# A graph attention layer with a routed expert layer: ScalarE's step in another order, and one penalty as a square

## What is computed

```python
# graph layer, on h = layernorm(x)
e_k   = leaky_relu((h * a_k) @ h.T, 0.2)          # k = 0..3
alpha = where(adj == k + 1, e_k, -9e15)           # one of four scores, or the penalty
x     = x + softmax(alpha) @ h
# expert layer, on layernorm(x): softmax gate over 16 experts, the best two,
# silu(x @ w1) * (x @ w2) @ w3 of each, weighted and added
```

## Time and profile before

| | |
|---|---|
| median of three runs | 921.12 us |
| profiled execution, its own time | 917.78 us |
| its span, first to last instruction | 915.6 us |
| TensorE busy | 732.7 us (80%) |
| VectorE busy | 518.6 us (57%) |
| GpSimd busy | 527.9 us (58%) |
| ScalarE busy | 382.3 us (42%) |
| mean granted TensorE clock | 0.939 |
| DMA | 133.26 MB, mean 146 GB/s |

### The profile page before, as it was taken

The page is one execution under the profiler, slowest core; times in us unless marked ns, Lnnn a source line. Parts: engine busy times, 40 slices in busy tenths (PEclk is TensorE's granted clock), DMA queues, the critical chain, the costliest instruction groups (busy, mean ns, idle before and its releaser), DMA issues.

```text
span 915.6 us, 17656 instructions
## 1 busy us (share of the span) xinstructions
PE 732.7 (80%) x4422; PEld 593.4 (65%) x4423; DVE 518.6 (57%) x1770; ACT 382.3 (42%) x947; POOL 527.9 (58%) x668
## 2 busy tenths in 40 slices
PE   4898988888898647887878878888788887888873
PEld 2455556555555536776767778777777777877873
DVE  4899999999999844444444444443333332333331
ACT  6878787878787212222222222222222222222220
POOL 3348877777777765554554554454564554544553
PEclk9999999999999858998999999999999998999987
DMA  5324453322221035766765544628755555555610
GB/s 151 93 81 143 120 145 119 110 85 90 87 83 34 28 112 173 216 202 209 233 210 180 165 163 147 208 95 245 226 174 182 179 178 187 168 163 173 205 58 1
DMA packets 127460, 133.26 MB, mean 146 GB/s; under 512 B 16362, under 2 KB 98545, under 8 KB 127378
## 3 DMA queue, kind: packets, MB, share of 16 engines
q1 hardware_dynamic: 107008, 94.66, 34.2%
q0 software_dynamic: 15616, 34.38, 11.0%
q10 hardware_dynamic: 4754, 3.25, 1.2%
HBM read 52.28 MB, written 41.19 MB: 102 GB/s over the span
## 4 chain that ended last, share of the span: by engine, by line
PE 64%; issue 17%; ACT 12%; another core or an unknown queue 3%; DVE 1%; POOL 1%; DMA 0%; POOLq 0%; ACTq 0%; DVEq 0%
PE psS L1124 30%; PE bank L1148 14%; ACT late L628 6%; PE bank L1040 4%; ACT late L636 4%; PE bank L1138 4%; PE psS L1012 3%; PE bank L1071 3%; PE bank L995 2%; PE bank L1024 2%; ACT h L645 1%; PE bank L1032 1%; POOL out_dram L593 1%; PE bank L1059 1%
## 5 line engine op out<-in xcount | busy, mean ns | idle before, releaser
L1124 PE MATMUL psS<-xT,late 128*128 128x256 f32 (+1 forms) x1280 | 269.9, 362 | 100.1 <-issue 87.0
L1124 PEld LDWEIGHTS psS<-xT,late 128*128 128x128 f32 x1280 | 213.0, 205 | 128.1 <-issue 98.5
L964 DVE TENSOR_TENSOR hid<-silu,psS 128x512 f32<-128x512 f32 x144 | 99.0, 687 | 239.5 <-PE psS L1124 108.4
L581 POOL DMA_INDIRECT second_list<-xin x144 | 142.4, 989 | 139.3 <-DVE xin L977 99.0
L593 POOL DMA_INDIRECT out_dram<-xin x144 | 141.5, 983 | 133.0 <-DVE xin L977 93.5
L667 ACT ACTIVATE silu<-psS 128x512 f32<-128x512 f32 x144 | 86.0, 597 | 298.7 <-PE psS L1124 171.6
L569 POOL DMA_INDIRECT first_list<-stage,slot x128 | 133.3, 1041 | 47.7 <-issue 36.0
L1148 PE MATMUL bank<-wts,hid 128*128 (+1 forms) x1152 | 159.7, 284 | 0.4 <-issue 0.3
L977 DVE SCALAR_TENSOR_TENSOR xin<-bank,xin 128x128 f32<-128x128 f32 x288 | 87.4, 345 | 109.5 <-remote 83.1
L1148 PEld LDWEIGHTS bank<-wts,hid 128*128 128x128 f32 x1152 | 148.1, 201 | 0.7 <-issue 0.7
L1012 PE MATMUL psS<-late,hT 128*128 128x512 f32 x256 | 117.4, 601 | 2.8 <-ACT late L628 2.8
(11 more groups left out here) (154 smaller groups left out, 812.5 us busy)
## 6 DMA issues: line engine op xcount, KB each, us to landing
late<-wts SPq DMA_DIRECT2D x160, 256.0 KB
xin<-second_list SPq DMA_DIRECT2D x48, 262.0 KB
X<-in_x_dram SPq DMA_DIRECT2D x32, 256.0 KB
late<-in_adj_dram SPq DMA_DIRECT2D x32, 256.0 KB
xin<-first_list SPq DMA_DIRECT2D x48, 134.0 KB
xin<-second_list SPq DMA_DIRECT2D x48, 131.0 KB
wts<-in_L_ffn_w_dram SPq DMA_DIRECT2D x48, 128.0 KB
xin<-first_list SPq DMA_DIRECT2D x48, 67.0 KB
```

The source lines that it names most:

```text
L581: pool.indirect_dma_start(second_list[:, :], bass.IndirectOffsetOnAxis(ap=xin[:, u, k, SLOT1:SLOT1 + 1].bitcast(i32), axis=0), xin[:, u, k ...
L964: v.tensor_tensor(hid[:, w, :], silu[:, w, :], psU[w], ALU.mult).then_inc(s_hid[u % TURNS], 1)
L1124: last = mm(out[:, c * W2 + rows.start:c * W2 + rows.stop], at[:, half * H + c * P:half * H + (c + 1) * P], xT[:, w, rows], start=True, st ...
```

## The change

ScalarE's order within a step: before it is `adjb(s)`, small exponential, `hT` and `hTa`, exponentials, `h(s+1)`, `probT`, `x1T`. Now it is small exponential, square, `hT` and `hTa`, exponentials, `adjb(s+1)`, `probT`, `x1T`, `h(s+1)`. So the bf16 copy of a group is made one step sooner, and `h` last.

The square: the penalty for k = 0 is made by ScalarE as `(2^28 * adj - 2^28)^2`, which is zero where `adj` is 1, read straight from the integer tile. VectorE makes the other three, as `(adj != k+1) * 2^56`. All four are positive now and TensorE subtracts them: the identity of the penalty matmul is replaced by its negative, `minusb`. The load of `adj` is released by the square's semaphore in place of the copy's.

```diff
-    NEG_INF = -9e15
+    ROOT = 2.0 ** 28
+    SQUARES = 1
...
             def load_adj(g):
-                wait(sp, s_adjb, g - 1)
+                wait(sp, s_squares, g - 1)
...
+            for k in range(SQUARES):
+                nc.gpsimd.memset(shift[:, k:k + 1], -ROOT * (k + 1)).then_inc(s_const, 1)
...
-                if on(0):
-                    act.wait_ge(s_adj[s % 2], (s // 2 + 1) * 16)
-                    wait(act, s_pen, s)
-                    nc.scalar.activation(adjb, adjt[:, s % 2, :], ACT.Copy).then_inc(s_adjb, 1)
                 if pair(s, 6) is not None:
...
+                if on(0):
+                    act.wait_ge(s_adj[s % 2], (s // 2 + 1) * 16)
+                    wait(act, s_S, s - 1)
+                    for k in range(SQUARES):
+                        last = nc.scalar.activation(pen[:, s % 2, k, :], adjt[:, s % 2, :], ACT.Square,
+                                                    scale=ROOT, bias=shift[:, k:k + 1])
+                    last.then_inc(s_squares, 1)
...
                 if on(-1):
                     g = s + 1
-                    act.wait_ge(s_sh, s + 2)
-                    wait(act, s_O, g - HB + 1)
-                    for t in range(T):
-                        last = nc.scalar.activation(h[:, g % HB, t * D:(t + 1) * D], X[:, g % XQ, t * D:(t + 1) * D],
-                                                    ACT.Identity, scale=norm[:, b, 0, t, 0:1],
-                                                    bias=norm[:, b, 0, t, 1:2])
-                    last.then_inc(s_h, 1)
+                    act.wait_ge(s_adj[g % 2], (g // 2 + 1) * 16)
+                    wait(act, s_pen, g)
+                    nc.scalar.activation(adjb, adjt[:, g % 2, :], ACT.Copy).then_inc(s_adjb, 1)
...
+                if on(-1):
+                    g = s + 1
+                    act.wait_ge(s_sh, s + 2)
+                    wait(act, s_O, g - HB + 1)
+                    for t in range(T):
+                        last = nc.scalar.activation(h[:, g % HB, t * D:(t + 1) * D], X[:, g % XQ, t * D:(t + 1) * D],
+                                                    ACT.Identity, scale=norm[:, b, 0, t, 0:1],
+                                                    bias=norm[:, b, 0, t, 1:2])
+                    last.then_inc(s_h, 1)
...
-                v.tensor_copy(identb[:, :], ident[:, :]).then_inc(s_base, 1)
+                v.tensor_scalar(minusb[:, :], ident[:, :], -1.0, None, ALU.mult).then_inc(s_base, 1)
...
-                    for k in range(K):
-                        last = v.tensor_scalar(pen[:, s % 2, k, :], adjb, float(k + 1), NEG_INF / SLOPE,
+                    for k in range(SQUARES, K):
+                        last = v.tensor_scalar(pen[:, s % 2, k, :], adjb, float(k + 1), ROOT * ROOT,
                                                ALU.not_equal, ALU.mult)
...
                     pe.wait_ge(s_pen, g + 1)
+                    pe.wait_ge(s_squares, g + 1)
                     for t in range(T):
-                        last = mm(psS[:, t, :], identb[:, :], pen[:, g % 2, :, t * D:(t + 1) * D],
+                        last = mm(psS[:, t, :], minusb[:, :], pen[:, g % 2, :, t * D:(t + 1) * D],
                                   start=False, stop=True)
```

More of the change, by code:

```diff
@@ L101, in gnn_then_moe @@
         pen = late[:, (K + 6) * C:(2 * K + 6) * C].bitcast(bf16).rearrange("p (q k c) -> p q k c", q=2, k=K)
-        identb = sb("identb", [P, P], bf16)
+        minusb = sb("minusb", [P, P], bf16)
         stats = sb("stats", [P, 2, 2, T, 3])
@@ L106, in gnn_then_moe @@
         norm = sb("norm", [P, 2, 2, T, 2])
+        shift = sb("shift", [P, SQUARES])
         minus_half = sb("minus_half", [P, 2, T])
@@ L235, in gnn_then_moe @@
         s_pen = sem("s_pen")
+        s_squares = sem("s_squares")
         s_sel = sem("s_sel")
@@ L295, in gnn_then_moe @@
         s_z = [sem(f"s_z{i}") for i in range(S)]
-        CONSTS = 10
+        CONSTS = 11
         AT = 2 * T * E
```

## The result

The changed kernel takes 914.26 us as the median of 17 runs (908.37 to 928.53), the kernel before 921.12 beside it (17 runs, 909.38 to 932.88). The ratio is 0.9936, with 95% interval 0.9909 to 0.9964: faster by 0.64%, where the forecast was 906.7, a ratio of 0.9843. The ratio is taken without the executions that ran over 1.5% above the fastest of their kernel, so it isn't the quotient of the two medians (0.9926). The time lies outside the forecast's range of 903.3 to 912.5. The profiled execution has a span of 912.4 us and took 914.26.

The account below looks back on a forecast made before the run. A TensorE-ScalarE loop bound the kernel, VectorE (8.80 us a step) was to bound it afterwards. Waits of 8.7 and penalties of 5.4 make 14.1; edges of −0.2 and +0.5 give 14.4 off 921.12: 906.7 us, range 903.3 to 912.5.

Parts of the forecast that it names:

- The loop: TensorE and ScalarE's cycle in a graph-layer step: short steps 8.50 us, long 9.04, mean 8.77, down 0.57.
- hT copy 0.67 later at 8.50: Short step: TensorE's transposes of h start at 7.83, ScalarE's hT copy follows at 8.50 us, against 8.97 before.
- the term of 8.7 us of waits taken out whole: VectorE's waits for TensorE's router product over 28 steps, 8.7 us, were all to disappear.
- VectorE as the bound at 8.80: After the change VectorE's own work, 8.80 us a step, was to set the pace, against 8.77 for the loop.
- Three penalties of 0.69: VectorE's penalties per step, three instead of four, were to last 0.69 us in all instead of 0.89.
- The square: ScalarE's square before the hT copy: 0.57 us, between 0.52 and 0.8, covered by the wait for the transposes.
- The wait of the adj copy: ScalarE's adj copy before probT newly needs VectorE's penalties of the same step; 1.4 us of room was to hold.
- Its signs of being right: Steps about 8.5 and 9.1 us, VectorE's router wait gone, L1040 0.66 sooner, square over before hT copy, three penalties 0.69.
- The rival of the covered gain: VectorE's internal gaps hide TensorE's lateness, so only the penalties come off: 5.4 us, median 915.7; chance 6%.
- The rival of GpSimd's late norm: GpSimd, making norm for h between scatters, becomes a brake: 2.3 us lost, median 909.0, up to 912.5; chance 20%.

Follow-up runs that it names:

- light: The changed kernel with GpSimd's two small copies of a step moved to ScalarE; 17.55 us a pair of steps, without late posts.
- order_only: The changed kernel without the square: ScalarE's new order kept, VectorE computes four penalties again; 17.85 us a pair of steps without late posts.
- square_only: The changed kernel with ScalarE's order of before, keeping the square ahead of hT and three penalties on VectorE; 18.67 us a pair of steps.
- micro_third: A kernel without the program or VectorE products: TensorE and ScalarE post beside GpSimd's scatters, transfers, memsets; TensorE's posts burst 0.9 us behind the last of four scatters.
- light_again: The changed kernel with GpSimd's two small copies moved to ScalarE, run again, this time with late posts; 18.04 us a pair of steps.

## Why the prediction was wrong in size

- **The loop: right without the hold.** Long step 9.04 forecast, 9.03 measured. Short step 8.50 forecast; 8.53 in the steps ahead of the scatters and wherever posts are not late.
- **The step that failed** is the one from the end of the transposes to the hT copy in a short step, "hT copy 0.67 later at 8.50". It took the transposes' 0.66 us as the whole of the distance. In the steps with scatters the posts are held, and it is 1.34 (199.62 to 200.96). The twelve short steps from 73.7 us on last 109.4 us together, where twelve of 8.53 are 102.4: 7.0 us more. That is the gap between the 14.4 us forecast and the 7.4 that came. In VectorE's account, from which the sum was made, it is the term of 8.7 us of waits taken out whole: 8.2 us of them are still there after the change, and light has next to none (0.3 us from 42 to 275). In three other executions the loss is of the same kind and somewhat smaller, 18.04 or 18.05 a pair instead of 18.18, and their first expert transposes come 9.1 us earlier than in the two profiles of the kernel before with late posts (means 321.72 and 330.86), where light without the hold comes 14.6 earlier.
- **VectorE as the bound at 8.80: neither shown nor refuted.** With four penalties its pace is 8.97 (order_only); one more penalty takes 0.21 us from start to start (0.81 for four, 0.60 for three), so with three it is some 8.76. The loop alone gives 8.78 (8.53 and 9.03). In light, without the hold, both fit: VectorE is never idle for over 0.04 us between 120 and 270 us, its reductions start 8.86 and 8.69 us apart, and the hT copy follows the transposes within 0.04 us in every step. With late posts VectorE isn't full: in the change it waits in every short step with scatters.
- **Three penalties of 0.69:** 0.68 to 0.69. **The square:** 0.72 instead of 0.57, inside the bounds, and covered (199.47 to 200.19, transposes until 200.28).
- **The wait of the adj copy** for penalties: none with the change, 4.8 us in order_only, where VectorE is slower.
- **Its signs of being right:** L1040's product (now L1054) starts 3.05 us behind the exponentials instead of 3.72, 0.67 sooner as forecast; the square is over before the hT copy. VectorE's wait before the router's scaling is not gone (8.2 us), and that was the sign that mattered.
- **The rival of the covered gain** (915.7, 6%) came closest to the 914.26 measured, by luck: by it only the penalties would pay, and it is the other way round, as square_only gained nothing and order_only 0.82 us a pair.
- **The rival of GpSimd's late norm** (909.0, up to 912.5, 20%) has a pair "with today's stretching", 18.11, that nearly meets the 18.18 measured, but by accident too: the norm of L561 is ready at 193.94 and h starts at 197.93, 3.99 us of room where there were 1.5 to 2.7 before. GpSimd has a part in it by its scatters, not by its pace.
- **What the trace of before had shown.** The router product's post came 0.40 us late in it, by the semaphore records, and TensorE's transposes of h ended just as the hold did. I read the waits by name and did not compare a wait's end with the end of the releaser's instruction. The two rows of the kernel before that stand under the result differ by it: the product ends at 205.03, the wait for it at 205.45. So in the short steps the wait that I put down to TensorE's lateness was the late post.

Open: why posts are late in some executions and not in others; and the changed kernel itself was never run without late posts, so that its pair there (between light's 17.55 and order_only's 17.85) is argued, not shown. Which resource the scatters and the posts share isn't settled either, and micro_third, the kernel without the program, ran only where late posts were about.

One rival is untested, and it bears on what a reader may carry away: that **the recording takes part in the hold**. In the eleven profiles with late posts, of the posts of TensorE, VectorE, ScalarE and GpSimd between 60 and 300 us 27% have no record (20% of TensorE's, 44% of ScalarE's); in the six without, 0.2%. Over the whole span the first profile of the change has 8,482 records of semaphores and light 17,360. In the kernel without the program, records are missing only beside scatters. So the executions with late posts are those whose records get lost, and since span and clock are on record for every execution, no run here tells whether the hold, or the 150 us between 767 and 915, would be there in an unrecorded one.

## What to carry to other kernels

A wait ends when the semaphore changes, not when the releaser's instruction ends: where a row's start lies well behind the end of what it waited for, look for what holds the post, here a row of indirect scatters on GpSimd. Before shortening a loop, see what then becomes due inside such a hold; work that becomes due in it gives the gain back, and here moving one engine's work only moved the meeting to another step. And compare a kernel only with one that ran beside it: the same code took 767 and 914 us on the same chip.

## What the runs showed of the hardware that I had not expected

- Indirect scatters of GpSimd hold back posts of TensorE until, as a rule, 0.66 to 0.98 us behind the end of the last one (some 240 of the 341 batches; of the others 57 come out 0.5 to 0.66 us behind the end of a third scatter and most of the rest about 1.2 behind it), in 11 of 17 profiles of the program; the other six have no late post between 60 and 300 us. Only TensorE's are held: no recorded post of VectorE or ScalarE in those eleven is over 0.11 us late.
- Late posts go with a longer expert phase. In the stretch from 450 to 700 us TensorE is busy 246.7 us in light and 207.5 in light_again, the same kernel. The waits of that stretch of light_again have two rows that are 1.6 and 0.6 us in light:

```profile
PEld psS L1138 <- issue: 44.6, 27, 4.2
PE psS L1138 <- issue: 37.0, 22, 4.0
```

- A scatter took 127.02 us beside back-to-back products of VectorE with two SBUF inputs, and 0.96 without them. The Trainium skill (SBUF — State Buffer, "SBUF: two separate sides") says that while VectorE runs an operation in a two-port mode, GpSimd is locked out of the port pair they share and cannot write a transfer's descriptors; operations with two SBUF inputs, it says, take the pair only against a GpSimd operation that reads SBUF. The trace agrees as far as it goes, with operations of the second kind: of 416 products of 0.42 us each the scatter sat through all that were left, and ended 0.84 us behind the last. That the ports are the cause no run here shows.
